# Filler matmuls on TensorE at the start and between stages, and one normalization moved ahead of a rotation

## The reference

```
x = x + attention_a(norm(x))   # one head of 128, rotary tables on q and k, softmax, no mask
x = x + experts(norm(x))       # 8 experts, top 1: softmax gate * (gelu(x W1[e] + b1[e]) W2[e] + b2[e])
x = x + attention_b(norm(x))   # 16 heads of 64, causal mask, output projection
x = x + experts(norm(x))       # the same weights as in the first expert block
```

## Time and profile before

| | |
|---|---|
| median of 3 runs | 865.49 us (863.0 to 867.37) |
| profiled execution, its own time | 865.85 us |
| its span in the trace | 863.5 us |
| PE busy | 789.8 us, 91% of the span |
| weight loads | 693.7 us, 80% |
| DVE, ACT, POOL busy | 622.7, 566.7, 440.4 us |
| chain that ended last, by engine | PE 75%, DVE 7%, POOL 7%, issue 6%, DMA 2%, ACT 1% |

### The profile page before, as it was taken

The page is one execution under the profiler, slowest core; times in us unless marked ns, Lnnn a source line. Parts: engine busy times, 40 slices in busy tenths (PEclk is TensorE's granted clock), DMA queues, the critical chain, the costliest instruction groups (busy, mean ns, idle before and its releaser), DMA issues.

```text
span 863.5 us, 24042 instructions
## 1 busy us (share of the span) xinstructions
PE 789.8 (91%) x6756; PEld 693.7 (80%) x6756; DVE 622.7 (72%) x2697; ACT 566.7 (66%) x2041; POOL 440.4 (51%) x771
## 2 busy tenths in 40 slices
PE   4999938999899999989999999999999999499992
PEld 3888827999778888878888888888778888399992
DVE  3889855666577777767777777887767776566664
ACT  1677645666577777767777777777767777266661
POOL 3334553677444454444544444544874544237772
PEclk9999957999999999999999999999999999889996
DMA  9920012313200000000000000000020000003135
GB/s 322 335 104 0 15 42 94 112 52 98 71 2 2 1 2 3 2 1 0 0 1 0 0 0 2 2 2 2 26 96 1 0 2 2 1 26 119 50 102 161
DMA packets 25928, 40.02 MB, mean 46 GB/s; under 512 B 4656, under 2 KB 17584, under 8 KB 24816
## 3 DMA queue, kind: packets, MB, share of 16 engines
q1 hardware_dynamic: 20848, 28.76, 10.4%
q0 software_dynamic: 4992, 10.27, 3.6%
HBM read 20.58 MB, written 18.43 MB: 45 GB/s over the span
## 4 chain that ended last, share of the span: by engine, by line
PE 75%; DVE 7%; POOL 7%; issue 6%; DMA 2%; ACT 1%; DVEq 0%; SPq 0%; POOLq 0%; ACTq 0%
PE PS L1151 11%; PE PS L1111 10%; PE PS L1163 10%; PE PS L1142 10%; PE PS L1120 9%; PE PS L1194 6%; PE PS L998 5%; PE PS L1000 5%; PE PS L999 5%; POOL xs_dram L323 2%; POOL w1b L356 1%; PE PS L1103 1%; PE PS L1048 1%; POOL pb L383 1%; POOL rstdA L318 1%
## 5 line engine op out<-in xcount | busy, mean ns | idle before, releaser
L381 POOL TENSOR_SCALAR pb<-pb,rib 128x128 f32<-128x128 f32 x256 | 96.1, 375 | 251.9 <-DVE rib L871 251.3
L862 DVE CUSTOM_DVE_ANT_0 PS<-PS,CST 128x128 f32<-128x128 f32 (+1 forms) x512 | 169.0, 381 | 65.3 <-PE PS L1163 62.0
L876 DVE COPY pT<-PS 128x384 f32<-128x384 f32 x256 | 139.7, 554 | 33.2 <-PE PS L1142 33.0
L522 ACT ACTIVATE pb<-PS,nbb 128x128 f32<-128x128 f32 x256 | 95.1, 371 | 102.4 <-DVE nbb L862 95.2
L496 ACT ACTIVATE yT<-PS,w1b 128x128 f32<-128x128 f32 x368 | 105.3, 369 | 64.8 <-PE PS L1111 64.8
L383 POOL TENSOR_SCALAR pb<-pb,rib 128x256 f32<-128x256 f32 x256 | 123.3, 482 | 0.0
L1142 PE MATMUL PS<-CST,pb 128*128 128x128 f32 x768 | 117.5, 279 | 4.4 <-POOL pb L383 3.6
L524 ACT ACTIVATE pb<-PS,nbb 128x256 f32<-128x256 f32 x256 | 121.4, 474 | 0.0
L339 POOL DMA_INDIRECT yt_dram<-XY x92 | 93.4, 1015 | 32.5 <-issue 19.7
L1142 PEld LDWEIGHTS PS<-CST,pb 128*128 128x128 f32 x768 | 85.8, 142 | 28.0 <-issue 15.3
L1151 PE MATMUL PS<-pT,vb 128*64 128x256 f32 (+1 forms) x1024 | 103.4, 339 | 1.9 <-DVE pT L876 1.6
(11 more groups left out here) (132 smaller groups left out, 1667.5 us busy)
## 6 DMA issues: line engine op xcount, KB each, us to landing
xs_dram<-XY SPq DMA_DIRECT2D x4, 1483.5 KB, 13.2
XY<-xs_dram SPq DMA_DIRECT2D x4, 1225.5 KB, 5.8
W1S<-in_W SPq DMA_DIRECT2D x1, 2048.0 KB, 21.3
W2S<-in_W SPq DMA_DIRECT2D x4, 512.0 KB, 8.3
out_dram<-X SPq DMA_DIRECT2D x8, 256.0 KB, 4.1
yt_dram<-XY POOLq DMA_INDIRECT x92, 2.4
XY<-xs_dram SPq DMA_DIRECT2D x4, 258.0 KB, 2.6
xs_dram<-TOK,POS POOLq DMA_INDIRECT x64, 2.4
```

The costliest lines, as they stand in the source:

```text
L862: last = nc.vector.tensor_tensor_reduce(ps, ps, CST[:, m:m + c1 - c0], -SCALE_B, HIGHEST, ALU.add, ALU.min, nbb[:, hh % 4, c0 // P:c0 // P ...
L876: nc.vector.tensor_copy(pT[:, hh % 4, :], PS[:, bank, 0:3 * P]).then_inc(b_pT, 1)
```

## The change

A bf16 tensor `idle` is set to zero by DVE as its first operation. A new function on TensorE, `keep_clock(n, bank)`, issues n matmuls of 128x128 zeros by 128x512 zeros into a PSUM bank that nobody reads at that time. It is called at the very beginning (20), after the steps 18, 19 and 20 of the first attention (7, 10, 10), in the first expert block after its route (20) and after the first three steps (6), in the last two steps of the second attention (11, 10), and in the second expert block after the first three steps (10). On DVE the normalization of batch 1 moves from behind the cosines of batch 0 to ahead of them.

```diff
--- before.py
+++ after.py
@@ -129,6 +129,7 @@
 
 
         X = sb("X", [P, NT, D])
+        idle = sb("idle", [P, 512], BF16)
         CST = sb("CST", [P, C_W])
         ident = CST[:, C_ID:C_ID + P]
         upperb = sb("upperb", [P, P], BF16)
@@ -221,7 +222,7 @@
         s_cst, s_x0, s_x1, s_wa, s_wb, s_wr, s_w1, s_w2, s_xs0 = (
             sem(n) for n in ("cst_in", "x_first_in", "x_rest_in", "w_attn_a_in", "w_attn_b_in", "w_router_in",
                              "w1_in", "w2_in", "xs_zeroed"))
-        s_castb, s_zero = sem("consts_cast"), sem("zeros_set")
+        s_castb, s_zero, s_idle = sem("consts_cast"), sem("zeros_set"), sem("idle_set")
 
         (a_xT_ps, a_xT, a_qk_ps, a_qks, a_sin, a_rot, a_rope, a_v_ps, a_v, a_scores, a_max, a_nb, a_exp, a_rinv, a_pT_ps, a_pT,
          a_out_ps, a_x) = (sem("a_" + n) for n in (
@@ -586,6 +587,7 @@
 
         @block.vector
         def _(dve):
+            nc.vector.memset(idle[:, :], 0.0).then_inc(s_idle, 1)
             dve.wait_ge(s_cst, 16)
             nc.vector.tensor_copy(upperb[:, :], CST[:, C_UP:C_UP + P])
             nc.vector.tensor_copy(onesb[:, :], CST[:, C_ONE:C_ONE + P])
@@ -674,6 +676,9 @@
                 if has(s):
                     norm_var(LN["A"], s, u)
                 part()
+                if fixed(s) and s == 1:
+
+                    norm_apply(LN["A"], s, TPB * s, u)
                 b = s - 1
                 if has(b):
                     dve.wait_ge(a_qk_ps, b + 1)
@@ -705,7 +710,7 @@
                     dve.wait_ge(a_max, b + 1)
                     nc.vector.tensor_scalar(nba[:, u, :], mxa[:, u, :], -SCALE_A, None, ALU.mult).then_inc(a_nb, 1)
                 part()
-                if has(s):
+                if has(s) and not (fixed(s) and s == 1):
                     if not fixed(s) or s >= 2:
                         dve.wait_ge(a_xT_ps, s - 1)
                     norm_apply(LN["A"], s, TPB * s, u)
@@ -999,6 +1004,11 @@
                 mm(ps, one_pass(lhs[0]), one_pass(rhs[1]), start=False, stop=False)
                 return mm(ps, one_pass(lhs[1]), one_pass(rhs[0]), start=False, stop=True)
 
+            def keep_clock(n, bank):
+
+                for _ in range(n):
+                    mm(PS[:, bank, :], idle[:, 0:P], idle[:, :], start=True, stop=True)
+
             def router_T(n, slot, bank):
                 pe.wait_ge(LN["F"]["s_out"], n + 1)
                 for i in range(TPB):
@@ -1122,7 +1132,12 @@
                         last.then_inc(f_y_ps, 1)
 
                 route(GROUPS * layer + 1)
-                expert_steps(pe, step, 0, first_quarter if layer == 0 else None)
+                keep_clock((20, 0)[layer], 4)
+                step(0, 0)
+                step(1, 1)
+                step(2, 2)
+                keep_clock((6, 10)[layer], 4)
+                expert_steps(pe, step, 3, first_quarter if layer == 0 else None)
 
             def first_quarter(i):
                 attn_b(0, 0, i, i + 1)
@@ -1217,6 +1232,8 @@
                         router_T(gb + NB, v, ONCE_BANK)
                     if q == 2 and has(gb):
                         router(gb + NB, v, ONCE_BANK)
+                        if fixed(s) and s >= NB + 1:
+                            keep_clock((11, 10)[s - (NB + 1)], T_BANK)
                     if q == 3 and has(s):
                         pe.wait_ge(LN["B"]["s_out"], s + 1)
                         for i in range(TPB):
@@ -1245,12 +1262,16 @@
                         scores(n, 0)
                         scores(n, 1)
 
+            pe.wait_ge(s_idle, 1)
+            keep_clock(20, 6)
             pe.wait_ge(s_cst, 16)
             pe.wait_ge(s_castb, 1)
             peeled(attn_a, 0, 8)
             turns(pe, attn_a, 8, ROUTE0_AT - 1)
             for s in range(ROUTE0_AT - 1, NB + 5):
                 attn_a(s, s % 2, (lambda: route(0)) if s == ROUTE0_AT else None)
+                if s >= NB + 2:
+                    keep_clock((7, 10, 10)[s - (NB + 2)], 4)
             experts(0)
             pe.wait_ge(f_y, 2 * NJ)
             pe.wait_ge(b_wl, 5)
```

## The result

The changed kernel takes 862.63 us (median of 11 runs, 860.36 to 864.09) against 865.49 us (11 runs, 863.0 to 869.31): ratio 0.9966, 95% interval 0.9952 to 0.9981. Its profiled execution took 863.25 us, with a span of 861.4 us. So it is faster, by 2.9 us in the medians and 2.6 in the profiled executions, where I had forecast 6.45.

The account below looks back on a forecast made before the run. It took TensorE at full clock to bound the expert blocks and second attention, leaving the start, first attention's end and expert-block starts open. -4.2 + 0 - 1.75 - 0.5 = -6.45 us on 865.85 gave 859.4 us; range 856.0 to 863.8.

Parts of the forecast that it names:

- Reading of the clock at the start: First projection ran at 1.2 GHz, judged by durations (3.75 against 1.99 us), although the granted-clock row showed 1.00.
- Rival 3: Start stays slow, because the clock row was right or the level is lost; only reordering counts there; 862.0 us, chance 0.12.
- The filler's length: One zero matmul on TensorE taken as 0.24 us at full clock and 0.48 at the low clock.
- Term 1: Start of the first attention: fast first projection and earlier normalization bring batch 1's cosines forward; -4.2 us, low end -2.6.
- rival 1: The clock falls once more in TensorE's gap after batch 1, giving back 1.6 us; 861.0 us, chance 0.27.
- Term 2, the tail: End of the first attention: chain is POOL's, so a faster TensorE clock gives 0, from -0.2 to +0.6 us.
- Term 3, the first expert block: First expert block: its first matmuls at full clock, gelu and third tile earlier; -1.75 us, ends -1.0 and -2.5.
- Term 4, the second: Second expert block: router product 0.51 instead of 1.02 us, the rest hidden behind DVE; -0.5 us, ends 0 and -1.5.
- No filler can help there: Expert blocks and second attention run on TensorE at full clock for most of the span, so fillers gain nothing there.

Follow-up runs that it names:

- e12: The changed kernel run once more, unaltered, on another chip for a second profile; ratio to the kernel before 0.9948, 908.2 us against 911.45.
- e10: The changed kernel without the 7, 10 and 10 fillers behind steps 18 to 20 of the first attention; ratio to the kernel before 0.9946.
- e7: e6 with 24 fillers at the start, 10 before the second attention, and DVE's steps 4 to 10 there written out; ratio 0.9878, 900.82 us.
- e2: The kernel before with only the 20 fillers at the start, no reorder and no later fillers; ratio 0.996.
- e6: The changed kernel with SyncE waiting for the second X load before it writes zeros to DRAM; ratio to the kernel before 0.9959, 907.53 us.
- e1: The kernel before with only batch 1's normalization moved ahead of batch 0's cosines, no fillers; ratio 0.9961.
- e3: The kernel before with only the later fillers, none at the start and no reorder; ratio 0.9987.
- e4: The changed kernel with its second X load split in two, 8 tiles first, then 20; ratio to the kernel before 0.9915, 858.05 us.
- e5: The kernel before with only DVE's memset of zeros added as first operation; single execution, -0.68 us between the cosines of batches 11 and 15.
- e8: The kernel before, unchanged, for a second profile; single execution, second X load landed at 15.6 us, second projection took 3.40 us.
- e9: The changed kernel with 13 more fillers between batch 1's v product and the third transposes; ratio to the kernel before 0.993, 907.57 us.
- e11: The changed kernel with split X load, 26 start fillers, 4 before the third transposes, and e7's other two edits; ratio 0.9849, 899.33 us against 911.45.

## Why the prediction was wrong, step by step

- **Reading of the clock at the start: right.** The first projection takes 1.96 us with fillers ahead of it and 3.75 without, while the row of the granted clock says 1.00 in both. Rival 3, which trusted the row, is out.
- **The filler's length: right within a tenth.** 0.43 and about 0.22 us, where I took 0.48 and 0.24. The first train ended at 8.2 us (forecast 7.9).
- **Term 1, the step that failed.** It said -4.2 us and measured -1.38 (-0.36 in e12). Two of its pieces were wrong. The load: I took 14.43 us from one profile as if it were fixed; it landed at 15.7, and this price is 1.3 us (cosines of batch 1 at 16.84 instead of 15.5). The clock: rival 1 priced one fall at 1.6 us behind an idle stretch of 1.9 us, with a chance of 0.27; the fall cost 1.5 us (-2.88 to -1.38). The price came out although its reason, that about half of the projection would run slow, gives only 0.9. The stretch became 3.5 us, 1.3 of it by the later load and 0.3 by a small operation of DVE (L711) that took 0.60 us instead of 0.17. With stretches of 3.5 to 3.9 us there the clock fell in all three profiles (the first of the changed kernel, e10, e12), with stretches of 1.9 to 2.1 in one of three (e7; not e2, e6), with stretches of at most 1.2 us in none of eight (before, e1, e3, e4, e5, e8, e9, e11). So with the usual landing rival 1 was the case to forecast. e4 and e6 bring the load earlier, e9 fills the idle stretch, and in all three the third projection is back at 1.99 us; in e7, with the load as early as in e6, the clock fell once more.
- **The parts do not add.** I summed the reorder and the fillers as one ladder ending at the load. e1 and e2 show that each alone reaches most of it: the reorder because it also closes the idle stretch before the second transposes, the fillers because they speed the first projection. Together they put TensorE ahead of the load by the stretch behind which the clock falls.
- **Term 2, the tail: right.** Zero, confirmed by e10. Unforeseen beside it: 0.7 us gained between batches 11 and 15 by the memset at the head of DVE's program (e5), and 0.66 us lost in a DMA of the last scatter, of which no experiment shows a cause.
- **Term 3, the first expert block: right.** -1.59 us (from -1.30 to -2.89) for -1.75, and -1.60 in e10.
- **Term 4, the second: right.** -0.42 at the router product and -0.16 behind it, for -0.5; DVE hid the rest as reckoned.
- **"No filler can help there", of the second attention: wrong.** The seams at 223 and 381 us, where the second attention begins and where DVE leaves its loop, hold idle stretches of 2.3 and 2.4 us, behind which the clock may fall. In the first pair of profiles they differ by 1.6 us against the changed kernel (-2.91 to -1.29). That is chance and not the change: behind the second seam the clock fell in the changed kernel's first profile and stayed up in e12, the same kernel, and of the kernel before it stayed up in the first profile and fell in e8. Of the twelve profiles with this seam it fell in four (also e3 and e10).

The measured 862.63 us lies inside my range of 856.0 to 863.8 and near rival 1's 861.0, in part by luck: the sum had no term for the fall in the second attention, the scatter's DMA or the memset. It also missed that one profile of before and the median of many hold different numbers of falls of the clock, so that it should have been made for an average of them.

## What to carry to other kernels

Before you sum several advances of the same ladder, look for the transfer that they all meet, and take its landing with a margin; past that point each further advance only becomes an idle stretch, and on TensorE an idle stretch can cost what was gained (here 1.5 us). Look in the trace for idle stretches of TensorE as long as those behind which the clock fell here (1.6 to 3.9 us), and treat those without a low clock behind them as a cost that happened not to fall due. Test the parts alone: one line moved (e1) brought as much as the whole change, and splitting the load on top of the change (e4) took it from 2.9 to 6.8 us.

## What the runs showed that I had not expected

The fall of the clock is not tied to an idle stretch of one length: of the stretches of 1.3 to 2.1 us ahead of the first three batches' transposes, the clock fell behind those of before (1.67), e8 (1.63), e4 (1.86) and e7 (1.87), and stayed up behind those of e2 (1.74 and 2.02) and e6 (1.57 and 2.05). Behind two equal stretches of 1.33 us it was up in e3 and had not come up at all in e5.

Multiplying zeros raises and keeps the clock like real work. With the 20 at the start the first projection takes 1.96 us instead of 3.75. The fillers follow each other every 0.43 us at the low clock (starts of their weight loads at 1.59 and 2.02 us) and every 0.22 us at the high one, where ten take 2.32 us from the first start to the last end, in the timeline of the changed kernel. By this the trace agrees with the 427 and 216 ns that the Trainium skill states (TensorE: Matmul & The Clock Gate, "Wait - 56ns, not 53.3ns?").

```profile
1.59 0.15 PEld L1010 LDWEIGHTS PS<-idle 128*128 128x128 bf16 x1 [0.27 <-issue]
...
2.02 0.15 PEld L1010 LDWEIGHTS PS<-idle 128*128 128x128 bf16 x1 [0.28 <-issue]
...
116.01 2.32 PE L1010 MATMUL PS<-idle 128*128 128x512 bf16 x10
```

DVE stood still for 3.0 to 3.3 us, waiting for nothing that the profile shows, on leaving its loop over the steps 4 to 7 of the second attention in all twelve profiles that have it, and not in the two where the steps are written out (e7, e11). Leaving its loop in the first attention shows 0.17 us of such idle time, so this is not the price of every loop. One more instruction at the head of DVE's program moved the work 80 us later by 0.7 us (e5); how is open.
